# An adaptive-norm transformer block on one core: the second norm's transposes ahead of the last two down products, the next queries ahead of the last gelu

## The chip, the core and the metric

The kernel runs on one core of one Trainium2 chip. The metric is the device time of the whole launch in microseconds (us); the median of three runs before the change is 1093.5 us, and they lie between 1090.59 and 1094.24. The core has five engines, each with an instruction queue of its own that runs strictly in order: TensorE (PE), VectorE (DVE), ScalarE (ACT), GpSimd (POOL) and SyncE (SP). They meet only at semaphores.

## What is computed

4096 tokens of 256 channels go through a linear attention with 16 heads, a residual, and a feed-forward part with one shared expert and the best two of eight routed experts:

```python
h = _layernorm(x) * (1 + ca) + sa
x = x + ga * attention(h)          # queries normed per head, times a 16 x 16 state per head, normed, @ Wo
h = _layernorm(x) * (1 + cb) + sb
shared = (gelu(h @ sw_up + sb_up) @ sw_down + sb_down) * 0.1
scores = sigmoid(h @ gate_w + bias); top_scores, top_idx = top_k(scores, 2)
combined = sum over the best two experts of w * (gelu(h @ up_w[e] + up_b[e]) @ down_w[e] + down_b[e]) * 0.1
out = shared + combined
x = x + gb * out / (max(abs(out)) + 1e-6)
```

## The kernel before

The launch is a row of blocks with a barrier between them: set-up of the weights, the keys and values (from which the states come), the attention and shared-expert stage, the routed experts, and the last residual. The change lies in the third of these.

That stage works on 8 groups of 512 tokens (4 tiles of 128). Matrices of float32 are split in two parts, high and low, and each product is three passes (high by high, high by low, low by high): ScalarE writes the high part, VectorE then subtracts to get the low part. `staggered` (L795) runs nine bodies, 0 to 8: body g does the attention of group g and, beside it, the shared expert and the routing of group f = g - 1. Body 0 has only the attention of group 0, body 8 only the shared expert of group 7. Bodies 3 to 6 are two turns of a hardware loop; the others are written out. I call the place where body g ends and body g + 1 begins boundary g. Each engine has its own `body`, and the order inside it is written by hand.

TensorE's body, in order: `norms()` (L820, the per-head sums of the squared queries, 16 small matmuls into PSUM tile psM; from group 2 on it waits at L824 until 20 (g - 1) routing steps are counted in `rt_dve`), `gate()` (L873, the gate's scores, which needs both parts of the transposed normed tokens h2T), then `chunk(0)` to `chunk(9)`, where `chunk(m)` is `up(m)` (L910, 6 matmuls of 512 columns into psU) and `down(m - 2)` (L923, 12 matmuls of 256 columns into psY), with the attention's own work between them: `outs`, `turn_gate`, `turn_z`, `attend`, `rank`. The last two chunks are `down(6)` and `down(7)` alone. Behind them stand `turn_h(0)` and `turn_h(1)` (L866): 8 transposes of the second norm's result h2 into psZ. They wait for `h2_ok`, which VectorE's `x_norm` counts up.

ScalarE's body: `score()` (the sigmoid of the gate's scores), `gelu(m)` for m = 0 to 7 (L996: a gelu and the cast to the high part), with the attention's two casts behind the fourth; then the next group's queries (L1027, L1028: `q5` and its square `qsq`), then `high` twice for h2T (L994).

VectorE's body: `norm_read` (L1046, waits for `norms`), `norm_inverse` (14 steps, each waiting for the one before), `gate_copy` (L1139), `out_read(0)`, `gate_read`, `low_g(0)` (L1125), `out_read(1)`, `low_g(1)`, `best`, `out_norm`, and so on to `x_read(1)`, `x_mean`, `low_g(5)`, `low_g(6)`, `x_norm` (L1110, 4 operations), `low_g(7)`, `place` (L1180, the routing's positions, the last six of its twenty counted steps, and behind them a sign to GpSimd), `shared_read` (L1195, waits for `down(7)`), `low_h(0)`, `low_h(1)` (L1120).

GpSimd's body: `rstd(0)` and `rstd(1)` (L1331, L1333, for the two norms), `scatter()` (L1340: waits for `place`, then 8 indirect DMAs out of h2), and `bias(g + 1)` (L1335, L1337: one addition over 128 x 1024 elements of X in SBUF). SyncE stores the shared expert's rows after `shared_read`.

Of the kernel before, what the change touches and what calls it, by code (L numbers as in the profile page):

```python
# [15 lines left out]
ACT = mybir.ActivationFunctionType  # L16
# [11 lines left out]
NG = NT // TG  # L28
# [5 lines left out]
MK = INNER // P  # L34
# [8 lines left out]
HALF = 512  # L43
# [19 lines left out]
def adaln_block(nc, x, Wq, bq, Wk, bk, Wv, bv, Wo, bo, ln_g, ln_b, gate_w, gate_b, up_w, up_b,  # L63
# [47 lines left out]
    expo = keep("expo", [P, 2, 128], F32)  # L111
# [22 lines left out]
    qT = att("qT", [P, CK, NT * P], F32)  # L134
# [560 lines left out]
    q5 = b2("q5", [P, CK, HALF], F32)  # L695
    qsq = b2("qsq", [P, CK, HALF], F32)
# [98 lines left out]
    def staggered(eng, body):  # L795

        body(0, 0, True, False)
        body(1, 1, True, True)
        body(2, 0, True, True)
        with eng.Fori(1, NG // 2 - 1) as i:  # L800
            body(2 * i + 1, 1, True, True)
            body(2 * i + 2, 0, True, True)
        body(NG - 1, 1, True, True)
        body(NG, 0, False, True)
# [3 lines left out]
    with ExitStack() as mem, nc.Block() as block:  # L808
# [8 lines left out]
        def _(pe):  # L817
            def body(g, q, att_on, ffn_on):
# [47 lines left out]
                def turn_h(k):  # L866
                    pe.wait_ge(h2_ok, TG * g + TG)
                    pe.wait_ge(tz_lo, 2 * g + 1 + k)
                    for t in range(TG):
                        mm = nc.tensor.transpose(psZ[:, k, t * P:(t + 1) * P], h2[:, q, t, k * P:(k + 1) * P], ident[:])  # L870
                    mm.then_inc(th_mm, 1)
# [23 lines left out]
                def rank():  # L895

                    pe.wait_ge(rt_oh, f + 1)
                    nc.tensor.matmul(psM[:, RANK:RANK + TG * E], tri[:], ohb[:].rearrange("p t e -> p (t e)"),
                                     start=True, stop=False, skip_group_check=True)
                    for t in range(TG - 1):  # L900
                        n = TG - 1 - t
                        nc.tensor.matmul(psM[:, RANK + (t + 1) * E:RANK + TG * E].rearrange("p (t e) -> p t e", e=E),
                                         one_b[:], ohb[:, t:t + 1].broadcast_to([P, n, E]), start=False,
                                         stop=(t == TG - 2), skip_group_check=True)
                    for t in range(TG):
                        mm = nc.tensor.matmul(psM[:, TOTAL:TOTAL + E], one_b[:], ohb[:, t], start=(t == 0),
                                              stop=(t == TG - 1))
                    mm.then_inc(rt_mm, 1)

                def up(m):  # L910
                    if later(f, 1) or m >= 2:
                        pe.wait_ge(u_g, MK * f + m - 1)
                    if m == 0:
                        pe.wait_ge(th_lo, 2 * f + 2)
                    n = 0
                    for k in range(CK):
                        for a, b in PASSES:
                            mm = nc.tensor.matmul(psU[:, m % 2], su[:, b, k, m * P:(m + 1) * P], h2T[:, r, a, k],  # L918
                                                  start=(n == 0), stop=(n == 5))
                            n += 1  # L920
                    mm.then_inc(u_mm, 1)

                def down(m):  # L923
                    pe.wait_ge(u_lo, MK * f + m + 1)
                    if m == 0 and later(f, 1):
                        pe.wait_ge(sh_ev, 2 * f)
                    for t in range(TG):
                        for n, (a, b) in enumerate(PASSES):
                            lhs = (ghi, glo)[a][:, m % 3, t * P:(t + 1) * P]
                            mm = nc.tensor.matmul(psY[:, t // 2, (t % 2) * C:(t % 2 + 1) * C], lhs, sd[:, b, m],  # L930
                                                  start=(m == 0 and t % 2 == 0 and n == 0),
                                                  stop=(m == MK - 1 and n == 2), skip_group_check=True)
                    mm.then_inc(d_mm, 1)

                def chunk(m):
                    if ffn_on:
                        if m < MK:
                            up(m)
                        if m >= 2:
                            down(m - 2)  # L940
# [28 lines left out]
                    attend(1)  # L969
                if ffn_on and att_on:  # L970
                    rank()
                for m in range(6, MK + 2):
                    chunk(m)
                if att_on:
                    turn_h(0)
                    turn_h(1)

            staggered(pe, body)

        @block.scalar  # L980
        def _(act):
            def body(g, q, att_on, ffn_on):
                f, r = g - 1, 1 - q

                def queries():
                    if later(g, 1):
                        act.wait_ge(o_mm, 2 * g)
                    src = qT[:, :, bass.ds(HALF * g, HALF)]
                    nc.scalar.activation(q5[:], src, ACT.Identity, bias=expo[:, 0, 0:1]).then_inc(q_pre, 1)
                    nc.scalar.activation(qsq[:], src, ACT.Square, bias=expo[:, 0, 0:1]).then_inc(q_pre, 1)  # L990

                def high(mm, out, dst, k):
                    act.wait_ge(mm, 2 * g + k + 1)
                    nc.scalar.copy(dst[:, 0, k], psZ[:, k]).then_inc(out, 1)  # L994

                def gelu(m):  # L996
                    act.wait_ge(u_mm, MK * f + m + 1)
                    if later(f, 1) or m >= 2:
                        act.wait_ge(u_lo, MK * f + m - 1)
                    nc.scalar.activation(gf[:, m % 2], psU[:, m % 2], ACT.Gelu, bias=sbu[:, m:m + 1]).then_inc(u_g, 1)  # L1000
                    act.wait_ge(u_g, MK * f + m + 1)
                    if later(f, 1) or m >= 3:
                        act.wait_ge(d_mm, MK * f + m - 2)
                    nc.scalar.copy(ghi[:, m % 3], gf[:, m % 2]).then_inc(u_hi, 1)  # L1004

                def score():
                    act.wait_ge(gt_ev, f + 1)
                    nc.scalar.activation(sc[:], lg[:], ACT.Sigmoid).then_inc(gt_sc, 1)

                if att_on and isinstance(g, int) and g == 0:  # L1010
                    queries()
                if ffn_on:
                    score()
                    for m in range(4):
                        gelu(m)
                if att_on:
                    high(tz_mm, tz_hi, zT, 0)
                    high(tz_mm, tz_hi, zT, 1)
                if ffn_on:
                    for m in range(4, MK):  # L1020
                        gelu(m)
                if att_on:
                    if not (isinstance(g, int) and g == NG - 1):
                        g2 = g + 1
                        act.wait_ge(o_mm, 2 * g2)
                        src = qT[:, :, bass.ds(HALF * g2, HALF)]
                        nc.scalar.activation(q5[:], src, ACT.Identity, bias=expo[:, 0, 0:1]).then_inc(q_pre, 1)  # L1027
                        nc.scalar.activation(qsq[:], src, ACT.Square, bias=expo[:, 0, 0:1]).then_inc(q_pre, 1)  # L1028
                    high(th_mm, th_hi, h2T[:, q], 0)
                    high(th_mm, th_hi, h2T[:, q], 1)  # L1030

            staggered(act, body)

            split_hi(act, 0, 0)
            act.wait_ge(sh_ev, 2 * NG)
            act.dma_start(shd_v[:, TG * (NG - 1):NT, :], sh[:]).then_inc(sh_st, 16)

        @block.vector
        def _(dve):
            def body(g, q, att_on, ffn_on):  # L1040
# [79 lines left out]
                def low_h(k):  # L1120
                    dve.wait_ge(th_hi, 2 * g + k + 1)
                    nc.vector.tensor_tensor(h2T[:, q, 1, k], psZ[:, k], f32(h2T[:, q, 0, k]), ALU.subtract
                                            ).then_inc(th_lo, 1)

                def low_g(m):  # L1125
                    if ffn_on:
                        dve.wait_ge(u_hi, MK * f + m + 1)
                        nc.vector.tensor_tensor(glo[:, m % 3], gf[:, m % 2], f32(ghi[:, m % 3]), ALU.subtract  # L1128
                                                ).then_inc(u_lo, 1)
# [112 lines left out]
                if att_on:  # L1242
                    x_norm()
                low_g(7)
                if ffn_on and not tail:
                    place()
                if tail:
# [3 lines left out]
                    shared_read()  # L1251
                if tail:
                    split_lo(dve, 0, 0)
                if att_on:
                    low_h(0)
                    low_h(1)


            tn = [0]
# [499 lines left out]
```

## Time and profile before

| | |
|---|---|
| median of three runs | 1093.5 us |
| the profiled execution, first to last instruction | 1092.4 us |
| attention and shared-expert stage in it | about 241 to 581 us |
| TensorE, VectorE, ScalarE, GpSimd busy in the whole span | 79, 58, 39, 26% |

A row of the timeline gives the start of an instruction (or of several like ones in a row, merged, "x4"), its time, engine, line and operation, what it writes and reads, and in brackets how long the engine had stood idle before it and what it had waited for. When rows are merged, the time runs from the first start to the last end. The end of a matmul is modelled, so for TensorE the starts are the better measure. An engine that is idle is no loss where it is not the one that others wait for.

### The profile page before, as it was taken

The page shows a single profiled execution, that of the slowest core. Times are in us where ns is not written, and L with a number is a line of the kernel's source. Part 1 is how long each engine was busy: PE and PEld are TensorE (multiplying, and loading weights), DVE is VectorE, ACT ScalarE, POOL GpSimd, SP SyncE. Part 2 cuts the span into 40 slices and gives each one's busy share as a digit, 9 for nine tenths or more (in the row PEclk, how much of TensorE's full clock was granted, in tenths as well). Part 3 has the DMA queues.
Part 4 walks back from the last instruction along what each step waited for, and adds up shares of the span by engine and source line. Part 5 has one row for each costly group of instructions (what it writes and reads, how often), then busy time and mean ns, then how long its engine had stood idle before and what let it go on. Part 6 is the DMA issues. An engine that isn't in the chain of part 4 may idle for free. (4 is left out here: it accounts for less than half of the span.)

```text
span 1092.4 us, 21618 instructions
## 1 busy us (share of the span) xinstructions
PE 865.6 (79%) x5961; PEld 784.7 (72%) x5962; DVE 633.4 (58%) x1513; ACT 425.3 (39%) x759; POOL 287.9 (26%) x258
## 2 busy tenths in 40 slices
PE   3358887963999988988983999999999999999200
PEld 1236766753788777877873999999999999999200
DVE  5878878746678777777864533443333333343147
ACT  0033333411444443544353555554455445554000
POOL 1420000011042343144240132333333333333315
PEclk9579999986899999999996999999999999999655
DMA  9200000000011011011038122522222223222152
GB/s 299 77 1 1 1 0 1 1 0 1 1 61 41 22 61 56 5 60 61 35 126 280 31 43 44 126 40 43 41 40 46 44 43 44 40 49 34 23 196 116
DMA packets 41220, 61.02 MB, mean 56 GB/s; under 512 B 6768, under 2 KB 33360, under 8 KB 41040
## 3 DMA queue, kind: packets, MB, share of 16 engines
q0 software_dynamic: 13952, 18.39, 10.0%
q1 hardware_dynamic: 21088, 33.30, 9.3%
q10 hardware_dynamic: 6128, 8.70, 2.4%
q8 instruction: 24, 0.39, 0.1%
q14 instruction: 28, 0.23, 0.1%
HBM read 31.81 MB, written 28.57 MB: 55 GB/s over the span
## 5 line engine op out<-in xcount | busy, mean ns | idle before, releaser
L1496 PE MATMUL psUp<-eT,wup 128*128 128x256 f32 x1632 | 207.4, 287 | 13.0 <-issue 9.2
L1496 PEld LDWEIGHTS psUp<-eT,wup 128*128 128x128 f32 x1632 | 200.8, 194 | 19.2 <-issue 18.8
L1516 PE MATMUL psE<-wdn,gTh 128*128 128x256 f32 x1088 | 198.1, 284 | 0.0
L1562 ACT ACTIVATE gu<-psUp,ubias 128x256 f32<-128x256 f32 x272 | 113.7, 469 | 192.8 <-PE psUp L1496 175.2
L1601 DVE TENSOR_TENSOR gTl<-gu,gTh 128x512 fp32r<-128x512 f32 x136 | 91.6, 691 | 155.5 <-ACT gTh L1567 112.8
L1516 PEld LDWEIGHTS psE<-wdn,gTh 128*128 128x128 f32 x1088 | 168.2, 191 | 0.0
L1650 POOL DMA_INDIRECT ffn_out<-yb,meta x68 | 112.7, 1658 | 171.3 <-DMA ffn_out<-yb,meta 100.6
L1516 PE MATMUL psE<-wdn,gTl 128*128 128x256 f32 x544 | 153.3, 282 | 0.0
L918 PE MATMUL psU<-h2T,su 128*128 128x512 f32 x384 | 104.6, 408 | 6.3 <-ACT gf L1000 6.3
L1516 PEld LDWEIGHTS psE<-wdn,gTl 128*128 128x128 f32 x544 | 103.6, 190 | 0.0
L930 PE MATMUL psY<-sd,ghi 128*128 128x256 f32 x512 | 94.9, 285 | 1.3 <-DVE glo L1128 1.1
L930 PEld LDWEIGHTS psY<-sd,ghi 128*128 128x128 f32 x512 | 80.8, 188 | 7.5 <-DVE glo L1128 4.7
L1567 ACT CAST gTh<-gu 128x512 fp32r<-128x512 f32 x136 | 84.3, 620 | 4.3
L918 PEld LDWEIGHTS psU<-h2T,su 128*128 128x128 f32 x384 | 70.0, 193 | 21.2 <-ACT gf L1000 7.7
L1344 POOL DMA_INDIRECT expert_in<-h,post x64 | 63.2, 987 | 67.7 <-DVEq L1193 50.7
L1611 DVE TENSOR_TENSOR yc<-psE,dbias 128x512 f32<-128x512 f32 x34 | 23.5, 692 | 93.1 <-PE psE L1516 87.8
L591 PE MATMUL psK<-wkq,hT 128*128 128x512 f32 x192 | 56.5, 431 | 25.8 <-DVE kraw L462 14.0
L1000 ACT ACTIVATE gf<-psU,sbu 128x512 f32<-128x512 f32 x64 | 44.1, 689 | 73.0 <-PE psU L918 70.8
L930 PE MATMUL psY<-sd,glo 128*128 128x256 f32 x256 | 72.3, 282 | 0.0
L1637 POOL DMA_DIRECT2D meta<-expert_in x34 | 26.2, 771 | 156.3 <-issue 156.3
L591 PEld LDWEIGHTS psK<-wkq,hT 128*128 128x128 f32 x192 | 36.0, 195 | 40.6 <-DVE kraw L462 18.7
L1128 DVE TENSOR_TENSOR glo<-gf,ghi 128x512 fp32r<-128x512 f32 x64 | 45.3, 716 | 27.6 <-ACT ghi L1004 27.6
(242 smaller groups left out, 1273.3 us busy)
## 6 DMA issues: line engine op xcount, KB each, us to landing
hin<-expert_in SPq DMA_DIRECT2D x36, 256.0 KB
X<-in_L_attn_x SPq DMA_DIRECT2D x8, 512.0 KB, 9.6
acc<-ffn_out SPq DMA_DIRECT2D x8, 512.0 KB, 5.0
out<-X ACTq DMA_DIRECT2D x8, 512.0 KB, 2.6
ffn_out<-sh SPq DMA_DIRECT2D x7, 512.0 KB, 3.0
raw_up<-in_L_ffn_up_w SPq DMA_DIRECT2D x3, 1024.0 KB, 6.0
raw_dn<-in_L_ffn_down_w SPq DMA_DIRECT2D x3, 1024.0 KB, 9.7
expert_in<-prow SPq DMA_DIRECT2D x8, 272.0 KB, 8.1
```

The lines of the kernel that those rows point to most:

```text
L591: mm = nc.tensor.matmul(psK[:], hT[:, q, a, k, t * P:(t + 1) * P], wkq[:, b, k, 0:KV * C], start=(n == 0), stop=(n == 3 * CK - 1))
L918: mm = nc.tensor.matmul(psU[:, m % 2], su[:, b, k, m * P:(m + 1) * P], h2T[:, r, a, k], start=(n == 0), stop=(n == 5))
L930: mm = nc.tensor.matmul(psY[:, t // 2, (t % 2) * C:(t % 2 + 1) * C], lhs, sd[:, b, m], start=(m == 0 and t % 2 == 0 and n == 0), stop=(m = ...
L1000: nc.scalar.activation(gf[:, m % 2], psU[:, m % 2], ACT.Gelu, bias=sbu[:, m:m + 1]).then_inc(u_g, 1)
L1128: nc.vector.tensor_tensor(glo[:, m % 3], gf[:, m % 2], f32(ghi[:, m % 3]), ALU.subtract).then_inc(u_lo, 1)
L1344: nc.gpsimd.indirect_dma_start(out=hs[:, :], out_offset=bass.IndirectOffsetOnAxis(ap=post[:, r, t, k:k + 1], axis=0), in_=h2[:, r, t], in_ ...
L1496: mm = nc.tensor.matmul(psU[:, c, (m % 2) * TR:(m % 2 + 1) * TR], wup[s][:, a, k, m * P:(m + 1) * P], eT[:, u, b, k], start=(n == 0), stop ...
L1516: mm = nc.tensor.matmul(psE[:, u, h * C:(h + 1) * C], (gTh, gTl)[a][:, u, m, h * P:(h + 1) * P], wdn[s][:, b, m], start=(n == 0), stop=(n ...
L1562: nc.scalar.activation(gu[:, c % 2, m], psU[:, c, m * TR:(m + 1) * TR], ACT.Gelu, bias=ubias[:, bass.ds(e * MK + 2 * c + m, 1)]).then_inc( ...
L1567: nc.scalar.copy(gTh[:, u, 2 * c:2 * c + 2], gu[:, c % 2]).then_inc(eu_hi, 1)
L1601: nc.vector.tensor_tensor(gTl[:, u, 2 * c:2 * c + 2], gu[:, c % 2], f32(gTh[:, u, 2 * c:2 * c + 2]), ALU.subtract).then_inc(eu_lo, 1)
L1650: nc.gpsimd.indirect_dma_start(out=shd[:, :], out_offset=bass.IndirectOffsetOnAxis(ap=meta[:, u, h, 0:1].bitcast(U32), axis=0), in_=yb[:, ...
```

## The change

In TensorE's body the two `turn_h` move from the end to between `down(5)` and `down(6)`. In ScalarE's body the next group's queries move ahead of `gelu(7)`, so that the two `high` follow `gelu(7)` directly. In VectorE's body the two `low_h` move from the end to directly behind `low_g(7)`, ahead of `place` and `shared_read`. No instruction is added or taken away.

```diff
--- before.py
+++ after.py
@@ -969,11 +969,13 @@
                     attend(1)
                 if ffn_on and att_on:
                     rank()
-                for m in range(6, MK + 2):
-                    chunk(m)
+                chunk(6)
+                chunk(7)
                 if att_on:
                     turn_h(0)
                     turn_h(1)
+                chunk(8)
+                chunk(9)
 
             staggered(pe, body)
 
@@ -1017,15 +1019,17 @@
                     high(tz_mm, tz_hi, zT, 0)
                     high(tz_mm, tz_hi, zT, 1)
                 if ffn_on:
-                    for m in range(4, MK):
+                    for m in range(4, MK - 1):
                         gelu(m)
-                if att_on:
-                    if not (isinstance(g, int) and g == NG - 1):
-                        g2 = g + 1
-                        act.wait_ge(o_mm, 2 * g2)
-                        src = qT[:, :, bass.ds(HALF * g2, HALF)]
-                        nc.scalar.activation(q5[:], src, ACT.Identity, bias=expo[:, 0, 0:1]).then_inc(q_pre, 1)
-                        nc.scalar.activation(qsq[:], src, ACT.Square, bias=expo[:, 0, 0:1]).then_inc(q_pre, 1)
+                if att_on and not (isinstance(g, int) and g == NG - 1):
+                    g2 = g + 1
+                    act.wait_ge(o_mm, 2 * g2)
+                    src = qT[:, :, bass.ds(HALF * g2, HALF)]
+                    nc.scalar.activation(q5[:], src, ACT.Identity, bias=expo[:, 0, 0:1]).then_inc(q_pre, 1)
+                    nc.scalar.activation(qsq[:], src, ACT.Square, bias=expo[:, 0, 0:1]).then_inc(q_pre, 1)
+                if ffn_on:
+                    gelu(MK - 1)
+                if att_on:
                     high(th_mm, th_hi, h2T[:, q], 0)
                     high(th_mm, th_hi, h2T[:, q], 1)
 
@@ -1242,6 +1246,9 @@
                 if att_on:
                     x_norm()
                 low_g(7)
+                if att_on:
+                    low_h(0)
+                    low_h(1)
                 if ffn_on and not tail:
                     place()
                 if tail:
@@ -1251,9 +1258,6 @@
                     shared_read()
                 if tail:
                     split_lo(dve, 0, 0)
-                if att_on:
-                    low_h(0)
-                    low_h(1)
 
 
             tn = [0]
```

## Rows read from the trace of the kernel before

**Rows 1.** The page's head: the span of the profiled execution.
```profile
span 1092.4 us, 21618 instructions
```
**Rows 2.** Timeline of TensorE at boundary 3: start, us, engine, line, operation, [idle before, releaser].
```profile
382.54 0.51 PE L930 MATMUL psY<-sd,ghi 128*128 128x256 f32 x2
...
386.91 1.04 PE L870 MATMUL psZ<-ident,h 128*128 128x128 f32 x8
387.78 1.85 PE L828 MATMUL psM<-heads,qsq 128*128 128x8 f32 x16
390.20 0.63 PE L881 MATMUL psU<-h2T,gw 128*8 128x512 f32 x2 [0.56 <-DVE h2T L1122]
```
**Rows 3.** Timeline of VectorE at boundary 3.
```profile
383.00 1.67 DVE L1117 SCALAR_TENSOR_TENSOR h<-z,rs,shift_b 128x256 f32<-128x256 f32 x4
...
385.19 0.18 DVE L1182 TENSOR_TENSOR rk<-psM,run 128x32 f32<-128x32 f32 x1
...
387.06 0.17 DVE L1191 CAST post<-pf 128x8 uint32<-128x8 f32 x1
387.57 1.29 DVE L1200 SCALAR_TENSOR_TENSOR sh<-psY,sbd_row 128x512 f32<-128x512 f32 x2 [0.34 <-DVE post L1191]
388.78 1.28 DVE L1122 TENSOR_TENSOR h2T<-psZ,h2T 128x512 fp32r<-128x512 f32 x2
389.98 0.21 DVE L1048 COPY nq<-psM 128x64 f32<-128x64 f32 x1
```
**Rows 4.** Timeline of ScalarE at boundary 3.
```profile
382.70 0.69 ACT L1000 ACTIVATE gf<-psU,sbu 128x512 f32<-128x512 f32 x1 [1.50 <-PE psU L918]
...
383.94 1.15 ACT L1027 ACTIVATE q<-qT,expo 128x1024 f32 x1
...
387.55 1.07 ACT L994 CAST h2T<-psZ 128x512 fp32r<-128x512 f32 x2 [1.41 <-PE psZ L870]
```
**Rows 5.** Boundary 0, where nothing stands ahead of the transposes.
```profile
268.83 3.75 DVE L1117 SCALAR_TENSOR_TENSOR h<-z,rs,shift_b 128x256 f32<-128x256 f32 x4
272.63 1.97 PE L870 MATMUL psZ<-ident,h 128*128 128x128 f32 x8 [7.24 <-DVE h L1117]
273.79 0.58 ACT L994 CAST h2T<-psZ 128x512 fp32r<-128x512 f32 x1 [12.55 <-PE psZ L870]
274.40 0.69 DVE L1122 TENSOR_TENSOR h2T<-psZ,h2T 128x512 fp32r<-128x512 f32 x1 [1.83 <-ACT h2T L994]
```
**Rows 6.** TensorE in body 4, the waits that end with VectorE's work.
```profile
395.43 0.38 PE L891 MATMUL psM<-ident,z 8*128 8x8 f32 x4 [1.39 <-DVE z L1142]
...
401.19 0.50 PE L930 MATMUL psY<-sd,ghi 128*128 128x256 f32 x2 [0.27 <-DVE glo L1128]
```
**Rows 7.** GpSimd's bias and VectorE's low_g(0) in body 3.
```profile
358.86 2.37 POOL L1337 TENSOR_TENSOR X<-X,bo_row 128x1024 f32<-128x1024 f32 x1
361.70 0.69 DVE L1128 TENSOR_TENSOR glo<-gf,ghi 128x512 fp32r<-128x512 f32 x1 [3.02 <-ACT ghi L1004]
```
**Rows 8.** The same two in body 4.
```profile
398.20 2.37 POOL L1337 TENSOR_TENSOR X<-X,bo_row 128x1024 f32 x1
399.96 1.18 DVE L1128 TENSOR_TENSOR glo<-gf,ghi 128x512 fp32r<-128x512 f32 x1 [3.02 <-ACT ghi L1004]
```
**Rows 9.** The same two in body 5.
```profile
436.71 2.38 POOL L1337 TENSOR_TENSOR X<-X,bo_row 128x1024 f32 x1
440.13 0.69 DVE L1128 TENSOR_TENSOR glo<-gf,ghi 128x512 fp32r<-128x512 f32 x1 [3.02 <-ACT ghi L1004]
```
**Rows 10.** Boundary 7, ahead of the body without attention.
```profile
536.98 1.67 DVE L1117 SCALAR_TENSOR_TENSOR h<-z,rs,shift_b 128x256 f32<-128x256 f32 x4
...
541.22 1.04 PE L870 MATMUL psZ<-ident,h 128*128 128x128 f32 x8
543.96 1.56 PE L881 MATMUL psU<-h2T,gw 128*8 128x512 f32 x6 [1.70 <-DVE h2T L1122]
...
545.56 0.68 DVE L1142 COPY z<-psU 8x512 f32<-8x512 f32 x1 [1.65 <-PE psU L881]
```
**Rows 11.** A stretch of body 3: PE, PEld, DVE, ACT, POOL busy, PEclk, DMA share, GB/s.
```profile
357.00:360.00 3.00, 2.82 (x13) 2.41 (x14) 1.47 (x6) 1.26 (x2) 2.67 (x3) 0.74 0.32 119
```

## The prediction

> **What bounds the kernel now.** I read the page's head first, for the span on which the sum is made: 1092.4 us, 1.1 us under the median of the three runs, 1093.5 [rows 1]. The change lies in one stage, so the next view is the timeline around one boundary, engine by engine. I took boundary 3; boundaries 1 to 6 have the same pattern, boundary 7 another, since no attention follows it.
>
> TensorE has hardly a pause there. From the start of `down(5)` at 382.54 to the transposes at 386.91 it does three down products, 1.46 us each; the transposes hand over to `norms` after 0.87 us, and the only gap is the 0.56 us before `gate`, at 390.20, put down to `low_h` [rows 2]. That gap is what the eye falls on. The question is what `gate` is needed for and what else comes late.
>
> VectorE answers it. Its row of work from `x_norm` (ends at 384.67) over `place` (385.19 to 387.23), `shared_read` (387.57), `low_h` (388.78) to `norm_read` (389.98) has one hole, of 0.34 us [rows 3]. Behind `norm_read` stand the 14 chained steps of `norm_inverse` and only then `gate_copy`. So TensorE, having done `gate` early, stands still 1.39 us for `gate_copy` and again a little before `down(0)`, for `low_g(0)` [rows 6]. The body is paced by VectorE from `norm_read` on, and the wait before `gate` is given back at once. `low_g(0)` itself comes 3.02 us after VectorE has run out of work, behind sigmoid and gelu [rows 8]: `norm_read`, `norm_inverse`, `gate_copy`, sigmoid, gelu, `low_g(0)` is one chain, and what delays its head delays its end, unless something else is later still.
>
> Something else is near: GpSimd. Its `bias` runs in body 4 from 398.20 to 400.57, and `low_g(0)`, which starts inside it at 399.96, takes 1.18 us and ends 0.57 us after `bias` [rows 8]. In bodies 3 and 5, where `bias` is over, the same operation takes 0.69 [rows 7, 9]. Bodies 2, 6 and 7 look like body 4: there too the end comes 0.55 to 0.57 us after that of `bias`. Read from the rows: this VectorE operation, with both inputs in SBUF, does not run while GpSimd's addition does.
>
> **The change part by part, on the clock of boundary 3.**
>
> *Transposes.* They wait for `x_norm`. Where nothing stands ahead of them they start 0.05 us after it: 268.83 + 3.75 = 272.58, then 272.63 [rows 5]. So they start at 384.67 + 0.05 = 384.72. `down(5)` is through at 382.54 + 1.46 = 384.00, so TensorE gets a new stall of 0.72 us. The two down products queued behind it end at 384.72 + 0.87 + 2.91 = 388.50. Before, all of this was over at 386.91 + 0.87 = 387.78: the order gives the stall to TensorE and saves none of its work.
>
> *Queries.* Two operations of ScalarE of about 1.1 us [rows 4]. ScalarE had been idle 1.50 us before `gelu(7)` at 382.70, so they run from 381.20 to 383.39 and `gelu(7)` starts 0.69 late; its cast ends at 384.73 instead of 384.04. `low_g(7)` starts at about 384.73 rather than 384.6. What covers this: `down(7)` now starts only at 387.0, and `low_h(0)` waits for the transposes anyway. ScalarE is free when these land. I count nothing. Without that cover it would be 0.1 us.
>
> *`low_h` ahead of `place` and `shared_read`.* From the start of the transposes to ScalarE's first cast it takes 387.55 - 386.91 = 0.64 us [rows 2, 4], from there to `low_h(0)` 274.40 - 273.79 = 0.61 [rows 5]. So `low_h(0)` starts at 384.72 + 0.64 + 0.61 = 385.97, where VectorE has stood idle for about 0.5 us, and the pair takes 388.78 to 389.98, 1.20 us [rows 3]. `place` starts at 387.17, not 385.19: 2.0 us late, and ends at 389.2.
>
> *The wait behind that.* From group 2 on `norms` waits at L824 for the routing steps of the body before, the last of which are in `place`. Before, they were done at 387.23, ahead of `norms` at 387.78; now they end at 389.2, after `down(7)`. So `norms`, with `gate` and all of TensorE's next body queued behind it, starts at 389.25 and ends 1.85 us later, at 391.10; by the distance of 0.35 us at most that `norm_read` had from the end of `norms` (389.63), it follows at 391.15 to 391.45. `shared_read` is no later: it starts 0.34 us after `place` and takes 1.21 us, to 390.75 [rows 2, 3]. I take 391.15, as VectorE's own work set the old distance. `norm_read` is 1.2 us late.
>
> *GpSimd.* `scatter` waits for `place`, its 8 DMAs and `bias` are queued behind, and it stands idle before: all of it moves by 2.0 us. `bias` of body 4 runs from 400.2 to 402.57. `low_g(0)` is ready at 399.96 + 1.2 = 401.15, almost 1 us into it. It ends at 402.57 + 0.57 = 403.14, not 401.14: 2.0 us late [rows 8]. In body 3 it is 361.23 + 2.0 + 0.57 = 363.80 instead of 362.39, 1.4 us [rows 7]. In body 5, 439.09 + 2.57 = 441.66 instead of 440.82, 0.85 us [rows 9]; that is behind the loop's jump, where the 1.2 us of the chain alone would make it about as much. Bodies 2, 6 and 7 repeat body 4. Behind `low_g(0)` stand `out_read(1)`, `rstd(0)` on GpSimd and the second half of VectorE's body, and TensorE's `down(0)`, all of which had waited for it before [rows 6]; I find no slack and pass the whole on. Sum: 4 x 2.0 + 1.4 + 0.85 = 10.25 us.
>
> The Trainium skill, page "SBUF — State Buffer", section "SBUF: two separate sides", says that a VectorE operation with two SBUF inputs and a GpSimd one that reads SBUF hold a port pair in turn, whichever starts first keeping it to its end. By its second half `low_g(0)` would lose nothing if it started ahead of `bias`; that is the second case below. The 1.18 against 0.69 us agrees with it as far as it goes.
>
> *Boundary 7.* No `norms` follow, and `gate` did wait: 1.70 us, until 543.96. Here the move pays. `x_norm` ends at 538.65, the transposes start at 538.70, `gate` after 0.87 + 2.91 us at 542.48, and ends by its 1.56 us at 544.04. VectorE does `low_h` from 539.95, `place` and `shared_read` until about 544.1, so `gate_copy` starts at 544.15 or 544.2 instead of 545.56 [rows 10]. TensorE had to wait for it, so the gain of 1.35 us goes through body 8, into the tables and the routed experts.
>
> Total: 1092.4 + 10.25 - 1.35 = 1101.3 us, and with the 1.1 us between that execution and the median 1102.4 us.
>
> **The rivals.**
>
> *The chain alone.* `low_g(0)` starts ahead of `bias`, or isn't held by it: then boundaries 1 to 6 cost only the delay of `norm_read`, 6 x 1.2 at most, about 0.8 to 0.9 where `place` is shorter or the loop's jump hides it, in sum 6.3. 1093.5 + 6.3 - 1.35 = 1098.4 us. Against it: three of the six starts fall inside `bias` by rows like those of body 4, and `bias` moves further than `low_g(0)` does. 13%.
>
> *The delay is absorbed.* VectorE's later work has slack that one timeline doesn't show, and only boundary 7 counts: 1093.5 - 1.35 = 1092.1 us. Against it: TensorE's waits for VectorE in rows 6. 10%.
>
> *TensorE paces the bodies.* Then the wait before `gate` is the loss, and removing it gains 6 x 0.56 + 1.70 = 5.1 us: 1088.4 us, faster. It decides from the point where TensorE's new stall of 0.72 us would be shorter than the wait saved, and where `gate_copy` comes before TensorE asks. The rows show 1.39 us the other way. 5%.
>
> *TensorE's clock.* In body 3 the granted clock was 0.74 over 3 us around the wait for `gate_copy`, which is 0.26 x 3 = 0.8 us of work lost if it paces [rows 11]; part of that stretch was at 1.2 instead of 2.4 GHz. In the other bodies the same work ran at 2.4 GHz. The stalls before `norms` and `down(0)` now grow. If each of the six bodies gets such a stretch, and passes it on, it is 1102.4 + 6 x 0.8 = 1107.1 us. 10%. [...]
>
> **How the numbers follow.** The forecast has 62%: 1102.4 us. The range reaches from 1096.5, under the second case with two bodies less, to 1107.0, the clock case; it leaves out the absorbed delay and the gain, 15%, and a little above. 0.3% is about what a measurement of this kernel can tell from no change, 3.3 us: faster is under 1090.2 (the last but one case and a bad draw of the third, 6%), within is up to 1096.8 (11%), slower has the forecast, the chain alone and the clock, 83%.
>
> **What would show it.** In the changed kernel's trace: transposes 0.05 us behind `x_norm`, with about 0.7 us idle before them; `norms` starting right behind the last step of `place`, not behind `down(7)`; `norm_read` 6.5 us after the end of `x_norm` (it was 5.3); `bias` starting some 2.0 us later after `x_norm`, and `low_g(0)` in bodies 2 to 7 ending 0.57 us after it, stretched to over 1.5 us; the periods from boundary 1 to 7 longer by 0.85 to 2.0 us; `gate` of body 8 without a wait. I would be wrong if `norms` didn't wait, if `low_g(0)` came at its short 0.69 us, or if the transposes found `x_norm` long done.

## The result and the profile after

The changed kernel takes 1100.9 us (median of 16 runs) against 1093.9 us for the kernel before (16 runs beside them): a ratio of 1.0061, 95% interval 1.0044 to 1.0079. It is slower, by 7.0 us; 1102.4 us was forecast, with a range of 1096.5 to 1107.0.

The page of the changed kernel begins with its span; that of before was 1092.4 us [rows 1].

```profile
span 1098.5 us, 21618 instructions
```

Timeline of TensorE at boundary 3, to be held against [rows 2] (start, us, engine, line, operation, idle before and releaser):

```profile
387.04 1.10 PE L870 MATMUL psZ<-ident,h 128*128 128x128 f32 x8 [0.49 <-DVE h L1121]
391.65 1.95 PE L828 MATMUL psM<-heads,qsq 128*128 128x8 f32 x16 [0.65 <-DVE post L1195]
393.46 1.55 PE L881 MATMUL psU<-h2T,gw 128*8 128x512 f32 x6
```

The gap ahead of `gate` is gone, and two others have taken its place: 0.49 us ahead of the transposes, waiting for `x_norm`, and 0.65 us ahead of `norms`, waiting for the last step of `place`. `norms` waits for `place` at all six boundaries with attention behind them, 0.34 to 0.78 us and some 3.5 us in sum, where the kernel before has no such wait.

VectorE at the same boundary, against [rows 3]:

```profile
385.32 1.67 DVE L1121 SCALAR_TENSOR_TENSOR h<-z,rs,shift_b 128x256 f32<-128x256 f32 x4
386.90 0.68 DVE L1132 TENSOR_TENSOR glo<-gf,ghi 128x512 fp32r<-128x512 f32 x1
388.35 1.29 DVE L1126 TENSOR_TENSOR h2T<-psZ,h2T 128x512 fp32r<-128x512 f32 x2 [0.77 <-ACT h2T L996]
389.56 0.18 DVE L1186 TENSOR_TENSOR rk<-psM,run 128x32 f32<-128x32 f32 x1
...
391.43 0.17 DVE L1195 CAST post<-pf 128x8 uint32<-128x8 f32 x1
391.94 1.29 DVE L1204 SCALAR_TENSOR_TENSOR sh<-psY,sbd_row 128x512 f32<-128x512 f32 x2 [0.34 <-DVE post L1195]
393.64 0.23 DVE L1052 COPY nq<-psM 128x64 f32<-128x64 f32 x1 [0.42 <-PE psM L828]
```

`x_norm` ends at 386.99. `place` ends 4.62 us after it (2.56 before), `norm_read` comes 6.65 us after it (5.31 before), 0.04 us behind the end of `norms`. The last row says who is late: TensorE's `norms`, no longer VectorE's own work.

And GpSimd's `bias` with VectorE's `low_g(0)` in body 4, against [rows 8]:

```profile
402.55 2.40 POOL L1341 TENSOR_TENSOR X<-X,bo_row 128x1024 f32 x1
403.52 1.99 DVE L1132 TENSOR_TENSOR glo<-gf,ghi 128x512 fp32r<-128x512 f32 x1 [3.02 <-ACT ghi L1006]
```

`low_g(0)` starts 16.53 us after `x_norm`, 1.2 us later than before, and ends at 405.51, 18.52 us after it, 2.05 us later: it takes 1.99 us instead of 1.18, and ends again 0.56 us behind `bias`.

At boundary 7, against [rows 10], `gate` follows `down(7)` without a wait, 3.83 us after `x_norm` instead of 5.31:

```profile
546.36 1.67 DVE L1121 SCALAR_TENSOR_TENSOR h<-z,rs,shift_b 128x256 f32<-128x256 f32 x4
548.08 1.09 PE L870 MATMUL psZ<-ident,h 128*128 128x128 f32 x8 [0.21 <-DVE h L1121]
551.86 1.56 PE L881 MATMUL psU<-h2T,gw 128*8 128x512 f32 x6
```

**Where the time is.** Two distances in the timelines measure the stage: from the end of `x_norm` in body 1 to that in body 7, which spans the six boundaries with attention behind them, and from there to the end of `low_g(7)` in body 8, which spans boundary 7.

| kernel (trace) | boundaries 1 to 7, us | boundary 7 on, us | both against before, us | runs: ratio to before | 95% interval |
|---|---|---|---|---|---|
| before | 228.6 | 29.3 | | | |
| before_again | 228.9 | 29.3 | | | |
| changed | 239.2 | 27.8 | +9.0 | 1.0061 | 1.0044 to 1.0079 |
| after_again | 239.2 | 27.9 | +9.1 | 1.0077 | 1.0050 to 1.0104 |
| place_first_2 | 229.9 | 27.9 | -0.3 | 0.9991 | 0.9963 to 1.0019 |
| low_h_last_2 | 235.8 | 32.2 | +9.9 | 1.0088 | 1.0055 to 1.0121 |
| bias_mid_after_2 | 243.6 | 27.9 | +13.4 | 1.0128 | 1.0099 to 1.0157 |
| bias_late_after | 234.5 | 27.9 | +4.4 | 1.0069 | 1.0042 to 1.0096 |
| bias_late_before | 232.5 | 29.3 | +3.7 | 1.0031 | 1.0005 to 1.0057 |
| best | 228.1 | 27.8 | -2.2 | 0.9969 | 0.9941 to 0.9996 |

("Against before" takes the mean of its two traces, 258.04 us, and sums not yet rounded.) The rest of the launch varies by more than some of these: behind `low_g(7)` of body 8 the same kernel before took 524.4 us in one trace and 519.5 in the other, the changed one 522.7 and 523.0. The span of the changed kernel is 6.1 us longer: 10.6 us lost in the bodies, less 1.5 us gained at boundary 7, less 1.2 and 1.7 us of such differences ahead of and behind them.

### The profile page after: what moved, and what is told of

It reads as the page before. It is cut to its first block and busy times, and to the rows that moved or that the text cites. A ratio compares the mean times of both kernels' runs of the same rounds, so it can differ in the third digit from the quotient of the medians.

```text
span 1098.5 us, 21618 instructions
## 1 busy us (share of the span) xinstructions
PE 868.7 (79%) x5961; PEld 784.9 (71%) x5962; DVE 637.1 (58%) x1513; ACT 424.6 (39%) x759; POOL 288.2 (26%) x258
## 5 line engine op out<-in xcount | busy, mean ns | idle before, releaser
L1132 DVE TENSOR_TENSOR glo<-gf,ghi 128x512 fp32r<-128x512 f32 x64 | 48.3, 764 | 28.3 <-ACT ghi L1006 28.2
```

## The experiments

Each of three batches ran on a chip of its own, always beside the kernel before. On one chip the kernel before takes 1107.8 us, on the other two 1095.9 and 1095.1; ratios are to the runs on the same chip. I call the first of them the slow chip. The first theory: the cost is `place`'s delay, which reaches VectorE's chain by two ways, the wait of `norms` at L824, and `scatter` and `bias`, which then hold up `low_g(0)`. The rivals: TensorE's new stall ahead of the transposes; the chain alone, with the stretch of `low_g(0)` hidden.

**The controls.** `before_again` and `after_again` have no edit.

> The kernel before, unchanged, for a trace from the same chip as the runs beside it. In the four experiments so far TensorE's semaphore increments between gate and up(1) came up to 5 us behind the ends of their matmuls, while the scatter's DMAs ran; in the trace of the kernel before they came within 0.1 us. If that belongs to the chip, this trace shows it as well on that chip, and the time is near 1107.8 us; if it belongs to the edits, this trace shows increments within 0.1 us, on whatever chip.

> The changed kernel, unchanged, on the same chip as the runs beside it. If the late increments belong to the chip and hit every kernel alike, the loss against the kernel before stays at 6 to 8 us; if they cover the place where the change costs, the loss shrinks.

`before_again`: 1094.4 us in one run, and a stage of 258.2 us against 257.9, the ends of `place`, `bias` and `low_g(0)` at boundary 3 to within 0.1 us. `after_again`: 1.0077, the changed kernel's stage to 0.1 us. So the two traces that the document began with repeat on another chip. Neither shows the late increments of the first batch (below), and neither do the later runs of three of the four kernels of that batch: they don't belong to the kernels.

**place_first: `place` ahead of `low_h`**

```diff
                 low_g(7)
+                if ffn_on and not tail:
+                    place()
                 if att_on:
                     low_h(0)
                     low_h(1)
-                if ffn_on and not tail:
-                    place()
```

> The changed kernel with place ahead of low_h again, so that only low_h and shared_read stand behind it. Theory (place's delay is what costs: it holds norms at L824 and pushes scatter and bias onto low_g(0)): place ends 2.2 to 2.6 us after x_norm as before the change, norms start about 3.9 us after x_norm (right behind down(7)), norm_read about 5.7 (before 5.3, changed 6.4 to 6.7), bias ends where it did before (15.2 to 15.9), and the 10.6 us that the bodies lost shrink to about 1 to 2 us; boundary 7 still gains 1.4 us. In all within 1.5 us of the kernel before. Rival A (TensorE's new stall ahead of the transposes costs, whatever VectorE's order is): the loss stays at 5 us or more. Rival B (half the loss is the wait of norms alone, GpSimd adds nothing): the same small loss, but bias_mid_after would then not gain.

> The same kernel as place_first. Where the increments come in time: within 1.5 us of the kernel before, bias ending 15.2 to 15.9 us after x_norm and norm_read 5.7 us after it, by the theory that place's delay is the cost; 5 us or more over it by the rival that TensorE's stall is.

The second run of it, on another chip, is 0.9991 of the time before. Its timelines of TensorE and VectorE at boundary 3, and of `bias` and `low_g(0)`:

```profile
392.63 1.10 PE L870 MATMUL psZ<-ident,h 128*128 128x128 f32 x8 [0.51 <-DVE h L1121]
396.44 1.85 PE L828 MATMUL psM<-heads,qsq 128*128 128x8 f32 x16
...
393.10 0.18 DVE L1186 TENSOR_TENSOR rk<-psM,run 128x32 f32<-128x32 f32 x1
394.97 0.17 DVE L1195 CAST post<-pf 128x8 uint32<-128x8 f32 x1
398.33 0.23 DVE L1052 COPY nq<-psM 128x64 f32<-128x64 f32 x1 [0.29 <-PE psM L828]
...
406.11 2.38 POOL L1341 TENSOR_TENSOR X<-X,bo_row 128x1024 f32 x1
408.15 0.89 DVE L1132 TENSOR_TENSOR glo<-gf,ghi 128x512 fp32r<-128x512 f32 x1 [3.02 <-ACT ghi L1006]
```

The stall ahead of the transposes is still there, 0.51 us, and of the 10.5 us that the six boundaries had lost 1.2 are left, which boundary 7 gives back with its 1.4. `norms` starts behind `down(7)` without a wait, `norm_read` 5.75 us after `x_norm`, `bias` ends at 15.91, `low_g(0)` at 16.47, where it ended before the change. The stall as the main cost is ruled out: with it, and with `place` in its old position, the kernel is as fast as before. What it does to `norm_read`, 0.4 us, is swallowed by `bias` in bodies 4, 6 and 7, where `bias` ends no later; bodies 2, 3 and 5 are 0.4 us longer each.

The first run, on the slow chip, was 1.0063 (1.0037 to 1.0089), a loss of the size that I had expected by the rival of the stall alone. But `norms` and `place` stood there as in the second run, and VectorE then waited in five bodies, 1.71 to 4.50 us, at `out_read(0)` for TensorE's `outs(0)`:

```profile
400.56 1.05 PE L839 MATMUL psO<-state,q 128*128 128x128 f32 x8
...
407.35 0.69 DVE L1074 TENSOR_TENSOR oz<-psO,nq 128x512 f32<-128x512 f32 x1 [4.47 <-remote]
```

The matmuls end at 401.61 by their records, and the semaphore they count up moves at 407.32; in the traces of other chips it moves within 0.1 us. All four kernels of that batch show such late increments while the scatter's DMAs run. What causes it is open, and so is whether the records or the increments are late; I read no cause out of that batch.

**low_h_last: VectorE's order as before the change, TensorE and ScalarE as changed**

```diff
                 low_g(7)
-                if att_on:
-                    low_h(0)
-                    low_h(1)
                 if ffn_on and not tail:
                     place()
...
                 if tail:
                     split_lo(dve, 0, 0)
+                if att_on:
+                    low_h(0)
+                    low_h(1)
```

> The changed kernel with VectorE's order as before the change (place, shared_read, low_h); TensorE's transposes and ScalarE's queries stay moved. Theory (VectorE paces, and the stall that TensorE takes ahead of the transposes moves shared_read and with it low_h and norm_read): place and bias end as before, shared_read starts about 4.1 us after x_norm (before 2.7 to 2.9), norm_read about 6.5, so 1.2 us later than before in bodies 2 to 7, which low_g(0) shows in full only where bias does not hold it: 0.9, 1.2, 0.7, 0.9, 0.7, 0.5 us, in sum about 5; and boundary 7 loses about 1.1 us instead of gaining 1.4. Time about 1099 to 1100 us. Rival (VectorE's reordering is the whole loss): 1092 to 1094 us.

> The same kernel as low_h_last. Where TensorE's increments come in time: norm_read 6.5 us after x_norm in bodies 2 to 7, behind shared_read and low_h; place and bias where they were before the change; low_g(0) ends 0.9, 1.2, 0.7, 0.9, 0.7, 0.5 us later than before, and boundary 7 loses 1.1 us: in sum 5 to 6 us over the kernel before. By the rival that VectorE's reordering is the whole loss it would be no slower than the kernel before.

1.0144 on the slow chip, 1.0088 (1.0055 to 1.0121) on another. There the stage lost 9.9 us where 5 to 6 had been expected: 7.1 us in the six boundaries and 2.9 us at boundary 7. `norm_read` is where it was expected, 6.44 to 6.57 us after `x_norm`, in five bodies, and at 7.29 in body 5, about where it was before the change:

```profile
392.68 1.29 DVE L1204 SCALAR_TENSOR_TENSOR sh<-psY,sbd_row 128x512 f32<-128x512 f32 x2 [1.60 <-PE psY L930]
393.89 1.28 DVE L1126 TENSOR_TENSOR h2T<-psZ,h2T 128x512 fp32r<-128x512 f32 x2
395.08 0.21 DVE L1052 COPY nq<-psM 128x64 f32<-128x64 f32 x1
```

`shared_read` waits for `down(7)`, which ends later with the transposes ahead of it: it starts 4.16 us after `x_norm` instead of 2.90, and `low_h` and `norm_read` stand behind it. What the stage lost beyond the expectation is TensorE's clock, as the rows read. `gate` now waits for `low_h`, and much of the work behind that wait runs slowly. TensorE at boundary 2, the windows around it (TensorE, its weight loads, VectorE, ScalarE, GpSimd busy, the granted clock, the DMA share and GB/s), and VectorE's `out_read(0)`:

```profile
355.08 2.60 PE L881 MATMUL psU<-h2T,gw 128*8 128x512 f32 x6 [0.97 <-DVE h2T L1126]
...
352.00:355.00 3.00, 2.11 (x20) 2.02 (x18) 2.54 (x5) 0.00 (x0) 2.39 (x3) 1.00 0.33 123
355.00:358.00 3.00, 2.92 (x8) 1.37 (x9) 2.59 (x13) 0.00 (x0) 2.08 (x4) 0.54 0.63 238
...
360.51 0.69 DVE L1074 TENSOR_TENSOR oz<-psO,nq 128x512 f32<-128x512 f32 x1 [0.71 <-PE psO L839]
```

`gate` takes 2.60 instead of 1.55 us at a granted clock of 0.54, most of the stretch at 1.2 instead of 2.4 GHz. `up(0)` and `outs(0)` come behind it, and VectorE, through with `norm_inverse` and `gate_copy`, waits 0.7 us for `outs(0)`. It does so in five of the six bodies, 0.25 to 0.76 us and 2.9 us in sum; in body 5, where `gate` takes 1.55 us, it doesn't. At boundary 7 `gate` and `up(0)` take 2.45 and 2.26 instead of 1.56 us each, 1.6 us together. The two sums are about what the stage lost beyond the expectation. So here the rival of the clock is real; no run takes the clock away alone. The rival that VectorE's reordering was the whole loss falls as it was put: all of it taken back costs more, and what has to come back is `place` alone (place_first_2). TensorE's move needs `low_h` to come early, ahead of `shared_read`.

**bias_mid_after and bias_mid_before: `bias` between the fifth and the sixth indirect DMA**

```diff
                                 in_=h2[:, r, t], in_offset=None).then_inc(scat, 16)
+                            if TOPK * t + k == 4 and att_on and not (isinstance(g, int) and g == NG - 1):
+                                bias(g + 1)
...
-                if att_on and not (isinstance(g, int) and g == NG - 1):
+                if att_on and not ffn_on:
                     bias(g + 1)
```

> The changed kernel with GpSimd's bias moved between the fifth and sixth of the eight indirect DMAs, about 5 us earlier. Theory (low_g(0) held by bias carries the difference between 1.1 to 1.4 and 2.0 us at each boundary): low_g(0) takes 0.69 us in every body, its start is unchanged after x_norm, and the periods shorten by what it was stretched and held: in bodies 2 to 7 about 0.7, 0.3, 1.3, 0, 1.3, 1.6 us, in sum some 5.2 us. Time about 1095.5 us against 1100.9. Rival (the chain of norms and norm_inverse alone sets the time, the stretch of low_g(0) is hidden): no change, 1100 to 1101 us. If bias lands on VectorE's norm_inverse instead, whose steps read two inputs of SBUF, those steps stretch and it gets slower.

> The kernel before with the same move of bias. Theory: low_g(0) is stretched before the change too, by 0.29, 0.49, 0.55 and 0.82 us in bodies 2, 4, 6 and 7, so this gains 2.1 us: about 1091.7 us against 1093.9. Rival (the stretch is hidden): no change.

> The same kernel as bias_mid_after. Where the increments come in time: low_g(0) takes 0.69 us in every body and the time is some 5 us under that of the changed kernel beside it, by the theory that bias holds low_g(0); equal to it by the rival that the chain alone sets the time.

Slower all three: 1.0065 and 1.0038 on the slow chip, 1.0128 (1.0099 to 1.0157) on another. In the second run `low_g(0)` does take 0.69 us in every body, but in bodies 2, 3 and 5 it starts 2.4 to 2.9 us later than in the changed kernel. Body 2:

```profile
320.62 3.04 DVE L1068 TENSOR_TENSOR nq<-nq 128x64 f32<-128x64 f32 x1
321.22 2.35 POOL L1341 TENSOR_TENSOR X<-X,bo_row 128x1024 f32<-128x1024 f32 x1
```

The last step of `norm_inverse`, usually 0.22 us, takes 3.04: it ends 0.09 us behind `bias`, though it started 0.60 us ahead of it by its record. In body 3 it takes 2.93, and in body 5 an earlier step of the chain takes 3.07. I had named the case that `bias` lands on `norm_inverse`, but not that a step which starts ahead of `bias` is held as well.

**bias_late_after and bias_late_before: one DMA later**

```diff
-                            if TOPK * t + k == 4 and att_on and not (isinstance(g, int) and g == NG - 1):
+                            if TOPK * t + k == 5 and att_on and not (isinstance(g, int) and g == NG - 1):
```

> The changed kernel with bias between the sixth and seventh indirect DMA. In bias_mid_after_2 it began 0.6 us after the last step of norm_inverse had started, and that step took 3.04 instead of 0.22 us; one DMA later it starts about 13.3 us after x_norm and ends at 15.7, past that step (ends 11.1) and ahead of low_g(0) (16.3 to 16.5). Theory: low_g(0) takes 0.69 us everywhere, the periods from boundary 1 to 7 are 0.7, 0.4, 1.3, 0, 1.3 and 1.6 us shorter than in the changed kernel, and the loss against the kernel before falls from 7 to 8 us to about 2 to 3 us. Rival (the stretch of low_g(0) is hidden behind the chain): 7 to 8 us as before.

> The kernel before with bias between the sixth and seventh indirect DMA: it starts 11.2 us after x_norm and ends at 13.6, between norm_inverse (ends 9.7) and low_g(0) (14.7 to 15.4). Theory: low_g(0) loses its stretch of 0.3, 0.5, 0.55 and 0.8 us in bodies 2, 4, 6 and 7, a gain of 2.1 us, 0.2%. Rival: nothing.

On the changed kernel no body is hit: every `low_g` of the trace takes 0.66 to 0.69 us, and the six boundaries take 234.5 us instead of 239.2. Body 4:

```profile
402.00 2.39 POOL L1341 TENSOR_TENSOR X<-X,bo_row 128x1024 f32 x1
...
405.88 0.69 DVE L1132 TENSOR_TENSOR glo<-gf,ghi 128x512 fp32r<-128x512 f32 x1 [3.02 <-ACT ghi L1006]
```

So the stretch was not hidden: without it the bodies are 4.7 us shorter, against 5.3 expected, somewhat under half of the 10.5 us that they had lost. In bodies 4 and 7 the gain falls short by 0.4 and 0.5 us: `up(0)` takes 2.76 and 2.50 us there instead of 1.55, and VectorE waits 0.30 and 0.37 us for `outs(0)`. The times of the runs don't show the gain: 1.0069 (1.0042 to 1.0096) against 1.0061 and 1.0077. The traced stage, 4.4 us over that of before, is 0.4%, just under the interval, and the traced execution, 1098.9 us, was the third fastest of 12, whose median is 1102.3. The trace decides on the mechanism; the gain in the whole is not shown.

On the kernel before, bodies 4, 6 and 7 gained about as expected, 0.5, 0.6 and 0.8 us of period against the mean of the two traces of before, body 2 gained 0.2, and bodies 3 and 5 lost 2.8 and 3.0:

```profile
361.52 3.03 DVE L1064 TENSOR_TENSOR nq<-nq 128x64 f32<-128x64 f32 x1
362.11 2.35 POOL L1337 TENSOR_TENSOR X<-X,bo_row 128x1024 f32<-128x1024 f32 x1
...
441.68 3.03 DVE L1062 TENSOR_SCALAR nq<-nq 128x64 f32<-128x64 f32 x1
```

Against the changed kernel with the same edit, `bias` comes about 2 us earlier here and `norm_inverse` only 1.0 to 1.3, and so it is still under way. In sum 1.0031 (1.0005 to 1.0057), slower. My expectation had `bias` start at 11.2 us after `x_norm` and `norm_inverse` end at 9.7. That is nearly so in body 4, where `bias` starts at 11.05; in body 3 `bias` starts at 10.0, and in body 5 `norm_inverse` is late: the step that is held, the last but two, starts only at 10.4.

**best: a version from what was found**

The changed kernel with `place` first, `bias` late, and the transposes between the last two down products:

```diff
                 chunk(7)
+                chunk(8)
                 if att_on:
                     turn_h(0)
                     turn_h(1)
-                chunk(8)
                 chunk(9)
```

> The changed kernel with place ahead of low_h, the transposes between down(6) and down(7) instead of ahead of both, and bias as in bias_late_after. Theory: no stall ahead of the transposes, norms start right behind down(7) 3.1 to 3.5 us after x_norm, norm_read 5.0 us after it where the loop's bodies are (before 5.3) and 5.3 elsewhere, low_g(0) unstretched, gate of body 8 at 3.5 us after x_norm instead of 5.3. Sum: 2.1 us for low_g(0), 4 x 0.3 for norm_read, 1.7 for boundary 7: 5 us under the kernel before, 0.995 of its time. Rival (the gain at one wait is taken back at the next, by TensorE's own work): 2 us or less.

0.9969 (0.9941 to 0.9996), 1093.9 against 1095.1 us in the medians: the only one of these shown faster than the kernel before, by 0.3%. At boundary 3 nothing waits any more on TensorE, and `norm_read` comes 5.20 us after `x_norm`:

```profile
391.43 1.03 PE L870 MATMUL psZ<-ident,h 128*128 128x128 f32 x8
393.73 1.85 PE L828 MATMUL psM<-heads,qsq 128*128 128x8 f32 x16
395.43 1.55 PE L881 MATMUL psU<-h2T,gw 128*8 128x512 f32 x6
```

The expectation had 5 us. The traced stage gained 2.2, 1.5 of them at boundary 7; `low_g(0)` is unstretched, but `norm_read` gained only 0.1 us in bodies 4, 6 and 7 and nothing in 2 and 3, and in body 5 `bias` again holds the last step of `norm_inverse`, for 3.04 us. Without those 2.8 us the stage would be some 5 us under that of before. That is worked out, not run.

## Why the prediction was right

*VectorE paces the bodies; the wait ahead of `gate` is no loss.* Shown. The wait went, and the kernel got slower. Throughout, the distance from the end of `low_g(0)` to that of the next `x_norm` stayed as it was, 20.5 us in bodies 1, 2 and 7, 22.3 in 3 and 5, 22.0 in 4 and 6, in the kernel before and the changed one: the delay of `low_g(0)` passed on whole, as the sum had it.

*Transposes 0.05 us behind `x_norm`, with a stall of 0.72 us.* 0.05 us, and 0.49 us at boundary 3 (0.19 at boundaries 1 and 2, 0.50 at 4 to 6). In the sum the stall was charged only through `down(7)`, and place_first_2, which has the stall and loses 1.2 us in the six boundaries, shows that this is nearly right.

*Queries ahead of the last gelu: nothing.* In the changed kernel `low_g(7)` follows `x_norm` as before, and ScalarE is idle 0.90 us before the casts for the transposes. It was not run alone.

*`place` 2.0 us late, `norms` held by it at L824.* 2.05 us at boundary 3; `norms` starts at 391.65, 0.05 us behind `place`'s last step. That the wait itself is what holds it was read from the row that names `place` and from place_first_2, where both go; the wait was not taken away alone, since it guards a tile that both use.

*`norm_read` 1.2 us late.* 1.35 us in bodies 4 and 6, 1.4 in body 7, 1.0 to 1.1 in bodies 2 and 3, 0.9 in body 5.

*`bias` 2.0 us late, `low_g(0)` ending 0.57 us behind it.* Ends 2.0 to 2.1 us later after `x_norm` in all six bodies, 0.56 or 0.57 us behind `bias` in five. In body 5 `low_g(0)` started 0.04 us ahead of the end of `bias` and was not held; the chain alone cost 0.9 us there. The 0.85 of the sum was worked out from a hold that didn't come, so its size is partly luck, though the prediction names the chain as a second way to it. The sign "stretched to over 1.5 us" came true in bodies 4, 6 and 7 only; bodies 2 and 3 took 1.37 and 1.02 us. And among the rivals the prediction counts three of six starts inside `bias`, where its own rows and words give four, bodies 2, 4, 6 and 7, in the kernel before; in the changed one all six are, body 5 by those 0.04 us. The six periods grew by 2.0, 1.6, 2.1, 0.9, 2.0 and 2.1 us: 10.6 us against 10.25.

*Boundary 7: 1.35 us gained.* 1.5 us; `gate` came 3.83 us after `x_norm`, the 3.83 of the working.

The stage lost 9.0 us, 8.9 were forecast. The step from span to launch was too small: the forecast adds 1.1 us, and in the runs that list both the launch is 1.6 to 1.7 us longer. The runs lost 7.0, with an interval from 4.8 to 8.6 us. Between those and the 9 us of both traces some 2 us are open: the other parts of the launch differ by up to 5 us from one trace to the next, and what they did in the untraced runs isn't known.

*The clock.* It had 10% as something on top of the forecast. The working says that outside body 3 the same work ran at 2.4 GHz; in the same trace body 5 has such a stretch too, with a granted clock of 0.50 from 437 to 440 us. In the changed kernel the granted clock fell at boundaries 1 and 2, to a mean of 0.56 from 316 to 319 us and 0.65 from 353 to 356, behind `norms`, ahead of which TensorE had stood idle 0.44 and 0.34 us; in after_again it fell at five of the six. VectorE then waited 0.30 and 0.13 us at `out_read(0)` for `outs(0)`, but `low_g(0)` was held by `bias` in the same bodies, and nothing of it is seen in the periods. The kernel before has one such wait in its second trace, 0.61 us in body 7, hidden in the same way. It does count where `bias` is out of the way, with 0.7 us in bias_late_after and 2.9 us in low_h_last_2. The mechanism was there, its effect was covered by a later one.

## What to carry to other kernels

A gap on the busiest engine is worth what the next thing needed is late by; follow the chain past the gap, on all engines, before removing it. When a step moves down its queue, list who waits for the steps it is moved past: here a small step of 2 us had two waiters on other engines, and the farther one, through eight DMAs and an addition, cost about as much as the near one. And an operation that holds up another engine's, as `bias` does here, has to be placed against the whole of that engine's row, with what starts shortly ahead of it, and not only against the operation that it was seen to hold.

## What the runs showed of the hardware

A VectorE operation whose record starts before that of GpSimd's addition can still be held until its end. It was seen 15 times, on all three chips, in five of the six traces with `bias` between two indirect DMAs, with a lead of 0.31 to 0.66 us by the records: the step took 2.77 to 3.11 us instead of 0.20 to 0.23 and ended 0.06 to 0.09 us behind the addition. Eleven were steps with two inputs in SBUF, four had a single input and constants (L1062 and L1066, 0.20 us otherwise). Steps that started 0.83 us ahead or more were not held; `bn_stats` and `bn_aggr`, with one input, ran beside `bias` in their usual time. Nor was a step held in body 0, where no indirect DMA stands ahead of `bias`: in all 14 traces the last step of `x_mean`, with two inputs in SBUF, starts 0.56 to 0.57 us ahead and takes its usual 0.48 us, and only `x_norm`'s first, 0.06 us behind the start of `bias`, is held. In the changed kernel:

```profile
265.77 1.64 DVE L1111 SCALAR_TENSOR_TENSOR z<-X,mv,scale_b 128x256 f32<-128x256 f32 x4
267.50 2.33 POOL L1341 TENSOR_TENSOR X<-X,bo_row 128x1024 f32<-128x1024 f32 x1
267.56 2.56 DVE L1121 SCALAR_TENSOR_TENSOR h<-z,rs,shift_b 128x256 f32<-128x256 f32 x1
```

The Trainium skill, page "SBUF — State Buffer", section "SBUF: two separate sides", has the one that starts first keep the ports; body 0 agrees with it, but by the records the 15 don't, and would only if the addition behind an indirect DMA takes the ports well ahead of its recorded start, which no run here tells.

On one chip of three, TensorE's semaphore increments came up to 5.7 us behind the recorded ends of their matmuls while indirect DMAs ran, and the kernel before was 1.1% slower there than on the others. What links the two, if anything, is open.
